# A mixture of experts whose outputs are written out to token rows, and a layer norm's root in one operation

## What is computed

```python
probs = softmax(xf @ Wg); topv, topi = top_k(probs, 2)      # 1024 tokens, 8 experts
gates = topv / sum(topv)
dest = where(pos < cap, eidx * cap + pos, e * cap)          # place in the expert's list, cap = 269
expert_in = buf.at[dest].set(repeat(xf, 2))                 # 8 x 269 rows
h = gelu(expert_in @ W1 + b1); y = h @ W2 + b2
out = sum over a token's 2 choices of gates * y[dest]       # nothing where there was no place left
layernorm(x) = (x - mean) / sqrt(var + 1e-5)                # ahead of each block
```

## Time and profile before

| | us |
|---|---|
| median of 3 runs (lowest, highest) | 455.98 (455.86, 456.38) |
| the profiled execution | 455.64 |
| its span, first to last instruction | 453.8 |
| TensorE busy in it | 382.8 (84%) |
| VectorE busy | 285.5 (63%) |
| ScalarE busy | 263.5 (58%) |
| GpSimd busy | 184.3 (41%) |

### The profile page before, as it was taken

How to read it: one execution, slowest core, us unless ns; L and a number is a source line. 1 busy time by engine, 2 the same in 40 slices (tenths; PEclk the granted TensorE clock), 3 DMA queues, 4 the chain that set the end, 5 groups by cost and what they waited for, 6 DMA issues and landing times. The chain is left out here.

```text
span 453.8 us, 10020 instructions
## 1 busy us (share of the span) xinstructions
PE 382.8 (84%) x3564; PEld 279.6 (62%) x3564; DVE 285.5 (63%) x859; ACT 263.5 (58%) x783; POOL 184.3 (41%) x294
## 2 busy tenths in 40 slices
PE   3779999999999999999962999714879999999943
PEld 1557877777777655566641899503556776777621
DVE  2155684887778797575661221149356676999995
ACT  3147567676777788778731643116466668565642
POOL 4493451443333531164473000178765353341131
PEclk9999999999999999999995899955569999999965
DMA  8992000000000030000002041111000000000001
GB/s 333 389 388 81 2 1 1 3 0 2 2 1 1 1 141 1 1 14 14 24 24 91 32 136 68 42 35 29 23 2 1 1 3 0 4 2 2 4 0 47
DMA packets 7136, 22.12 MB, mean 49 GB/s; under 512 B 1215, under 2 KB 3503, under 8 KB 6575
## 3 DMA queue, kind: packets, MB, share of 16 engines
q1 hardware_dynamic: 6063, 19.38, 11.7%
q0 software_dynamic: 1024, 2.10, 1.6%
HBM read 14.60 MB, written 6.88 MB: 47 GB/s over the span
## 5 line engine op out<-in xcount | busy, mean ns | idle before, releaser
L498 ACT ACTIVATE prob<-bank,mx 128x128 f32<-128x128 f32 x256 | 81.3, 384 | 22.9 <-DVE mx L1209 20.1
L1209 DVE TENSOR_REDUCE mx<-bank 128x4 f32<-128x512 f32 x96 | 63.9, 683 | 30.0 <-PE bank L783 21.1
L418 POOL TENSOR_TENSOR prob<-prob,rden 128x512 f32<-128x512 f32 x32 | 33.4, 1050 | 60.0 <-DVE rden L1231 60.0
L391 POOL TENSOR_SCALAR rstd<-mv 128x1 f32<-128x1 f32 x64 | 12.9, 201 | 78.1 <-DVE mv L1184 74.9
L393 POOL TENSOR_TENSOR rstd<-rstd,minus_half 128x1 f32<-128x1 f32 x72 | 41.7, 580 | 6.0
L483 ACT ACTIVATE probT<-bank 128x512 f32<-128x512 f32 x64 | 38.4, 622 | 8.5 <-PE bank L810 8.2
L810 PE MATMUL bank<-pack,prob 128*128 128x128 f32 x256 | 39.2, 278 | 1.2 <-ACT prob L498 0.5
L438 POOL DMA_INDIRECT moe_rows<-yrows_d,row_of x16 | 15.8, 989 | 52.3 <-DMA yrows_d<-o_n 48.3
L810 PEld LDWEIGHTS bank<-pack,prob 128*128 128x128 f32 x256 | 28.6, 141 | 10.2 <-issue 5.0
L412 POOL TENSOR_SCALAR xn<-pack,mv,rstd 128x128 f32<-128x128 f32 x32 | 27.1, 846 | 5.9 <-POOL rstd L393 5.4
L498 ACT ACTIVATION_READ_ACCUMULATOR prob<-bank,mx 128x1 f32 x128 | 27.5, 215 | 0.0
(11 more groups left out here) (235 smaller groups left out, 977.8 us busy)
## 6 DMA issues: line engine op xcount, KB each, us to landing
yrows_d<-moe_rows SPq DMA_DIRECT2D x2, 1510.0 KB, 21.1
pack<-pack_d SPq DMA_DIRECT2D x1, 2112.0 KB, 15.9
expert<-experts_d SPq DMA_DIRECT2D x4, 514.0 KB, 8.6
pack<-experts_d SPq DMA_DIRECT2D x4, 514.0 KB, 5.3
pack<-pack_d SPq DMA_DIRECT2D x1, 2048.0 KB, 10.6
xrows_d<-moe_rows SPq DMA_DIRECT2D x1, 1080.0 KB, 21.2
moe_rows<-xrows_d SPq DMA_DIRECT2D x8, 135.0 KB, 2.7
yrows_d<-o_n SPq DMA_DIRECT2D x8, 135.0 KB, 1.8
```

What stands on the lines that cost most here:

```text
L418: pool.tensor_tensor(part, part, r.to_broadcast([P, GH, P]), ALU.mult).then_inc(E[A0]["norm"].sem, 1)
L498: act.activation(prob[:, g % 2, P * j:P * j + P], bank[S_BANK[g % 2]][:, P * j:P * j + P], ACT.Exp, bias=mx[:, g % 2, j:j + 1], **kw).then ...
L1209: dve.tensor_reduce(out, bank[S_BANK[g % 2]][:, :].rearrange("p (h t) -> p h t", h=GH), AX.X, ALU.max, negate=True).then_inc(E[layer]["max ...
```

## The change

*Sends.* A routed row gets two more numbers: the token's first target row in `yrows_d` and its first expert. The target area now holds two rows a token, in the order of tokens, with spare rows behind for places that no token took. `send_to` on VectorE works out from the loaded rows where each of an expert's rows belongs (choice one or two), and `send` on GpSimd scatters the expert's output there, three scatters of 90 rows an expert. When all are in, SP loads a batch's rows with one plain transfer each. The gathers go, and so do SP's stores.

*Root.* The statistics get a third group, set once: count 0, mean 0, and a spread that aggregates to the small constant. So the variance comes out with the constant in it, and `rs` needs the power alone. `rs_hid` likewise; `rms_hid` stays as it was.

*Keys.* Three expert buffers move from `pack1` to `pack3` (the raw feed-forward weights, free once they are made ternary). So `kt[1]` is free earlier; `keys3` and `fold` on TensorE and `k4_sb` stand ahead of the experts now, and the exp of the gate weights (`route_exp`) ahead of the experts' gelu.

*Order.* All tables of numbers are new. *Start:* one zeroing of `yrows_d` of 1 MB takes the place of two of 1.5 MB, and the zeroing waits for a constant that is copied in.

```diff
-        expert = [expert2[:, n, :] for n in range(2)] + [packed[1][:, EXPERT * n:EXPERT * n + EXPERT] for n in range(EXPERT_BUFS - 2)]
+        expert = [expert2[:, n, :] for n in range(2)] + [packed[3][:, EXPERT * n:EXPERT * n + EXPERT] for n in range(EXPERT_BUFS - 2)]
...
+        x_row = moe_rows[0:SP_, :].rearrange("p (e c n) -> p e c n", e=NE, c=SC)
+        row_tok = x_row[:, :, :, P]
+        row_first = x_row[:, :, :, P + 1].bitcast(U32)
...
             for e in range(NE):
-                wait(sp, MOE, "y_sb", Item(e, e))
-                sp.dma_start(yrows[e, 0:SLOT, :].rearrange("(p c) d -> p (c d)", c=SC), y_out[0:SP_, e % 2, :]
-                             ).then_inc(y_stored[e % 2], 16)
                 if e + EXPERT_BUFS < NE:
                     wait(sp, MOE, "y", Item(e, e))
                     load_expert(e + EXPERT_BUFS)
+            for k in range(2):
+                sp.wait_ge(y_sent[k], 16 * SC * (NE // 2))
+            for b in range(B):
+                sp.dma_start(y_got[:, b, :, :].rearrange("p k d -> p (k d)"),
+                             yrows_d[TOPK + TOPK * P * b:TOPK + TOPK * P * (b + 1), :].rearrange("(p k) d -> p (k d)", k=TOPK)
+                             ).then_inc(y_loaded[b], 16)
...
-                inverse_root(rstd[layer][:, k, 0:1], mv[layer][:, k, 1:2], scale, eps, ev, it, 1)
+                pool.tensor_tensor(rstd[layer][:, k, 0:1], mv[layer][:, k, 1:2], minus_half, ALU.pow).then_inc(ev.sem, 1)
...
-            def fetch(b):
-                for j in range(TOPK):
-                    pool.indirect_dma_start(y_got[:, b, j, :], None, yrows_d,
-                                            bass.IndirectOffsetOnAxis(ap=row_of[:, b, j:j + 1], axis=0)
-                                            ).then_inc(y_fetched[b], 16)
...
+            def send(it, c):
+
+                if c == 0:
+                    wait(pool, MOE, "to", it)
+                wait(pool, MOE, "y_sb", it, 2 if c == SC - 1 else 1)
+                pool.indirect_dma_start(yrows_d, bass.IndirectOffsetOnAxis(ap=y_to[0:SP_, it.b, c:c + 1], axis=0),
+                                        y_out[0:SP_, it.k, P * c:P * c + P], None).then_inc(y_sent[it.k], 16)
...
+            for part, value in ((every_stats[:, :, :, STATS:STATS + 2], 0.0), (every_stats[:, :, :, STATS + 3:2 * STATS], 0.0),
+                                (every_stats[:, 0:7, :, STATS + 2], P * LN_EPS), (every_stats[:, 7, :, STATS + 2], P * RMS_EPS * LN_EPS),
+                                (every_stats[:, 8, :, STATS + 2], F * LN_EPS)):
+                dve.memset(part, value).then_inc(stats_ready, 1)
...
+            def send_to(it):
+
+                dve.wait_ge(x_loaded[it.b], 16)
+                dve.scalar_tensor_tensor(y_to[0:SP_, it.b, :], row_first[:, it.b, :], float(it.b), row_tok[:, it.b, :], ALU.is_equal,
+                                         ALU.add).then_inc(E[MOE]["to"].sem, 1)
...
-                    dve.wait_ge(y_stored[it.k], 16 * (it.b // 2))
+                    dve.wait_ge(y_sent[it.k], 16 * SC * (it.b // 2))
...
-            walk(stages, [(11.6, masks), (288.3, first_fetches)])
+            walk(stages, [(-52.8, masks)])
```

## The result

The changed kernel takes **440.93 us** (median of 4 runs, 440.70 to 443.10) where the kernel before took 455.92 in the same comparison (455.72 to 456.38): a ratio of **0.968, interval 0.9649 to 0.9712**. The span of the profiled execution is 439.1 us instead of 453.8. Forecast were 441.0 and 433 to 449; sum and milestone came out as worked out, but not by the path worked out.

A forecast was written before the change was run, and what follows sets the result against it. From 300 to 340 us TensorE ran near half clock, mostly idle until 310, while GpSimd's gathers and norms paced the batches. 455.64 - 14.2 (milestone) - 0.6 (root) = 440.8, with 0.34 for the median 441; range 433 to 449.

The forecast's parts named there:

- The sends are hidden, just: Expert stage: 24 GpSimd scatters at 1.26 us; 21 fit between first and last expert sum, 26.5 of 29 us.
- rival "slower": Expert stage: sends that hold GpSimd longer don't fit; gain used up from 1.9 us each, 462 us at 2.2; chance 0.05.
- +0.85 behind the last sum: Last expert's sum to first token sum: three scatters and a load take 7.3 us, 6.45 before, so 0.85 us later.
- Keys at the entry, "0": Entry to the experts: first input copy 2.3 us late, set against a possible clock rise halving 5.0 us of matmuls; net 0.
- Nearly without a break: Entry to the experts: work filling the gap before them is nearly unbroken, the reason given for taking 0.
- the bound of +2.3: Entry to the experts: upper bound for late copy and clock together, 2.3 us later; the lower bound was -0.2.
- the wait for gelu: End of the experts: last down-projection must wait for the last hidden matmuls' gelu, 0.49 us, with hand-overs +0.9.
- Half clock until 320: A2 to milestone: TensorE at half clock until 320 us, then 5.9 us of work at full clock, nine tenths busy: milestone 326.
- The 5.5 us that the first batch lay behind the keys are in this, and the rest is the gathers: A2 to milestone: the 14.2 us gain contains 5.5 us from moving the keys, the rest from removing the gathers.
- the rival *More: Clock rises by 312 and experts start at full clock: milestone at 320, time 435 (430 to 437.5); chance 0.18.
- The root, -0.6: Layer norms: one GpSimd operation fewer, felt on the last batch into routing and the last at the end: -0.6 us together.
- Table loads, no term: ScalarE: two fewer loads up to the milestone, 2.6 us off an engine that isn't the bound; counted as nothing.

The follow-up runs named there:

- The keys split: Changed kernel, but VectorE makes four of its eight keys, then the first expert's input copy, then the rest; keys use two other banks: 439.19 us, again 438.09.
- the keys behind the maximum: Changed kernel with keys and fold put back behind the last expert, VectorE's keys behind the first maximum of A2: 447.87 us, ratio 0.9815.

## Why the prediction was right, and where it was not

The time was right, 440.9 for 441, and in part by luck. The first transpose of A2 came 3.1 us later than worked out (304.2 for 301.1); from there to the milestone it took 2.2 us less; and behind the milestone 1.4 us went, for which the forecast had no source but the root.

- **The sends are hidden, just:** right. 1.23 us a step (1.26 taken); GpSimd waited 7 us in all for sums (5.2 of it beyond the usual 0.30 between two sends), and eight more scatters came out 4.7 us late. That also bears out the slope of the rival "slower". The 24 took 0.92 to 0.95 us each beside VectorE's copies and sums. The Trainium skill (SBUF — State Buffer, section "SBUF: two separate sides") would have them held up where VectorE is in a two-port mode; no run here shows that.
- **+0.85 behind the last sum:** right in sum. 7.29 us from the last sum's end to the first token sum, 7.3 worked out. Within it the third send started 3.07 us behind the sum (2.3 taken), and the first load landed in 2.0 us (2.7 taken).
- **Keys at the entry, "0":** this step failed. The copy was late as said (251.26; 250.8 worked out), but the clock did not pay for it. TensorE worked through to 247.5 and the clock rose at 247.1; then TensorE waited 3.07 us for that very copy, the clock fell at 250.6 (both by stretches of 1 us), and the next matmuls ran at half. "Nearly without a break" overlooked the wait that the same paragraph had just priced. So the bound of +2.3 came true: the first expert matmul stood 2.2 us later, counted from the routing's end, and the first sixteen records of hidden matmuls took 7.2 us from there, as before (251.83 to 259.01; 249.06 to 256.23). In all the experts ended 3.5 us later by that count, where 0.9 was expected; the wait for gelu was 0.67 of it, and 0.6 lies elsewhere in the experts. The routing's end itself came 0.56 us later. The keys split, which takes the late copy away, gave 2 to 4 us back.
- **Half clock until 320:** mis-sized twice. The clock rose at 312, 8 us behind the first transpose, not 19 (one condition of the rival *More*); but from there to the milestone TensorE was busy 77% of the time (11.47 of 14.9 us), not nine tenths. From first transpose to milestone it took 22.7 us, 24.9 worked out (25.5 by the terms as they stand: 320 and 6.6 are 326.6, not 326). Milestone 326.9.
- **"The 5.5 us that the first batch lay behind the keys are in this, and the rest is the gathers":** the keys right in size, the sum wrong. Beside the sends the keys' move is worth 4.7 us, beside the gathers -1.5. There GpSimd's 4.35 us a batch hid the keys. With the keys still in A2 the rest of the change brings 8.4 us, with them gone 1.5 + 13.2 = 14.7.
- **The root, -0.6:** nothing that can be measured. It isn't on routing's way either: the last routing matmul came at 241.61, after 241.05. The span behind the milestone did shrink, from 113.6 to 112.2 us, but with the two-operation root it is 112.2 as well, so the root is not the cause. It moves with other edits too (114.2 with the keys behind the maximum); what sets it stays open.
- **Table loads, no term:** no run undid them, so their worth stays open. But "an engine that isn't the bound here" was no reason: two of the three loads left between A2's start and the milestone stand in waits of TensorE, the second just ahead of the milestone. ScalarE, then TensorE, in the changed kernel:

```profile
306.30 1.28 ACT L558 ACT_TABLE_LOAD   x1 [1.29 <-DVE mx L1262]
...
323.83 1.28 ACT L558 ACT_TABLE_LOAD   x1
```

```profile
308.10 0.47 PE L929 MATMUL bank<-pack 128*128 128x128 f32 x1 [1.83 <-ACT pack L558]
...
325.63 0.33 PE L929 MATMUL bank<-pack 128*128 128x128 f32 x1 [1.47 <-ACT pack L558]
```

In the kernel before, the load at 329.14 stands in such a wait of 2.25 us.

## What to carry to other kernels

Work that is moved into a gap must be cut so that the first instruction behind the gap still comes on time: one late copy cost its own 2 us, and with it the clock rose late in all five profiles, which in the split kernel was worth another 1.9. A repair can be worth nothing by itself and much beside another one of the same stage, when the limit that the other takes away hides it; undo each alone, and do each alone, before the gain is shared out. When a total comes out right, check its terms.

## What was not expected of the hardware

The granted clock is not a property of the code alone. The same order took the first hidden matmuls at half clock in one execution and at full in another (the split kernel, twice), 1.9 us apart at the last sum. The two ran on different chips; but on one of them alone the mean clock of the split kernel's six runs lay between 0.933 and 0.952, and their times between 436.54 and 440.41 us. And from 30 to 40 us the clock was 1.00 or 0.83, with which the routing's end moved by 1 to 2.7 us; both were seen on one chip, in kernels with the same order up to there (1.00 with the keys split, 0.83 in the changed kernel's second profile).

Keeping TensorE busy through a wait did not pay in the one kernel that tried it for A2. With eleven matmuls ahead of A2 the clock was still full at its first transpose, fell in the thin first batch (1.67 of 5 us busy) and came back at 316.5 us, where it had come back at 310.0 and 308.5 in the two profiles of the kernel that had idled.
